# Two masked graph-attention layers: the second layer without complements, every key tile in the form of indicator and mask

## The chip, the cores and the metric

The program runs on one NeuronCore of a Trainium2 chip. Its engines work side by side and each takes its instructions in order: TensorE (PE in the profile, its weight loads PEld), VectorE (DVE), ScalarE (ACT), GpSimd (POOL) and SyncE (SP), which issues the transfers. They wait for one another through semaphores. The metric is the device time of one execution in microseconds, the median of several.

## What is computed

Eight batches of 2048 nodes with 256 features go through two attention layers over one adjacency matrix. The change touches the second layer alone:

```python
q = (h @ W).reshape(B, N, H, D)                       # H = 4 heads, D = 64
e_src = jnp.einsum('bnhd,d->bnh', q, a_src)
e_dst = jnp.einsum('bnhd,d->bnh', q, a_dst)
e = e_src[:, :, None, :] + e_dst[:, None, :, :]
e = jnp.where(e >= 0, e, ALPHA * e)                   # ALPHA = 0.2
e = jnp.where(mask, e, NEG_INF)
attn = jax.nn.softmax(e, axis=2)
h_prime = jnp.einsum('bijh,bjhd->bihd', attn, q)
return jax.nn.elu(h_prime.reshape(B, N, H * D))
...
x = x + _L1_gnn_ref(h, adj, L1_gnn_W, L1_gnn_a)       # h = relu(layernorm(x))
```

## The kernel before

Three blocks run one after the other: the mask is turned and cast, layer 0 works until about 3950 us, then `layer1_block` runs, of which this text tells.

**The idea of layer 1.** The exponential of a leaky ReLU of a sum falls into products: where e_src + e_dst is positive the weight is a factor of the query times a factor b of the key, elsewhere another factor of the query times a factor s of the key. So for each head the kernel needs two masked sums over keys: over the pairs with a positive sum, with q times b, and over the other neighbours, with q times s. Each q row has a column of ones added (E1 = 65 columns), whose sum gives the denominator. TensorE forms both sums; the query factors are multiplied on afterwards.

**Tiles.** A batch `b` has 8 units `m`: head `m // 2`, half `m % 2` of the queries (1024 queries, HT = 8 tiles of 128). A unit has 16 steps `j`, one for each key tile of 128. Eight batches make 64 units and 1024 steps.

**One step.** ScalarE writes `cond` (L1116), which is huge where the sum is positive and 0 elsewhere; two buffers. VectorE takes the minimum with the mask (`pick`, L1277): `u`, 1 for a neighbour with a positive sum; a ring of four buffers. TensorE uses pieces of 128 columns of `u` as stationary operand and the weighted keys as moving one, accumulating in PSUM (`sums`, two sets, one for each half). The weighted keys are float32 values split into a high and a low fp16 part, so each product is done twice.

There are two kinds of key tiles. On an **even** tile VectorE also forms the complement `u2` = mask - u (`rest`, L1285, issued at step j + 1 behind that step's pick). TensorE does per query tile u times b (high, low) and u2 times s (high, low), four matmuls of 65 columns (L1006). On an **odd** tile there is no complement, since (mask - u) s = u (-s) + mask s: two matmuls of 130 columns with u against [b, -s] (L1011) and two of 65 with the mask against s (L1015). Both kinds load 32 stationary tiles a step. A tensor `sign` of 1 and -1 makes s negative on odd tiles (`sign_b`, L1244).

**Building the weighted keys.** For each head VectorE multiplies q by b and by s into `x32` (`weigh`, L1252, at steps 10 and 11), ScalarE rounds to fp16 at step 14 (`high`, L1093 for even tiles, L1094 for odd), VectorE subtracts to get the low parts (`low`, L1260, L1263, at steps 2 and 3 of the next unit) and turns -s back to s for the mask's part (`back`, L1268, step 4). This is done in units m = 6, 7, 0 and 1 for the heads to come.

**What else stands in the loop.** Of the unit before: denominators, `weighted` (the eviction from PSUM, L1326 and L1329, step 8), `value_plus_one` (L1336, step 9), ScalarE's exponential (L1123, step 14, behind `high`), the ELU (L1342, step 14 on VectorE) and the addition to the output (L1350, step 15). In units m = 1 to 5 the projections of the next batch are made in four strips: TensorE transposes at steps 8 and 11 and projects (L975) at 12, 15, 0 and 3, ScalarE copies the results, VectorE takes the statistics. The order is written by hand in the functions `batch` of each engine. VectorE's pick waits for the ring, that is for TensorE's step four before it; ScalarE's comparison waits for the pick two before it. TensorE, VectorE and ScalarE each jump back once a batch (TensorE at L1049).

Of the kernel before, what the change touches and what calls it, by code (L numbers as in the profile page):

```python
# [18 lines left out]
ALU = mybir.AluOpType  # L19
# [4 lines left out]
F16 = mybir.dt.float16  # L24
# [677 lines left out]
PLAIN = 4  # L702
MIXED = 6
PAIRS = NT // 2
# [7 lines left out]
def layer1_block(nc, x1, w, a, out, mask_dram, s_dram, d_dram):  # L712
    with ExitStack() as ctx:
# [39 lines left out]
        sign = sb("sign", [P, NT, H])  # L753
# [7 lines left out]
        u2 = sb("u2", [P, RING // 2, HALF], F16)  # L761
# [5 lines left out]
        v1 = sb("v1", [P, HT, D])  # L767
        e = sb("e", [P, HT, D])
# [35 lines left out]
        u2_ready = sem("u2_ready")  # L804
# [119 lines left out]
        def _(pool):  # L924
# [6 lines left out]
            nc.gpsimd.memset(sign[:, 0:NT:2, :], 1.0)  # L931
            nc.gpsimd.memset(sign[:, 1:NT:2, :], -1.0)
# [18 lines left out]
        def _(pe):  # L951
# [34 lines left out]
            def step(b, m, j):  # L986
# [6 lines left out]
                if j % 2 == 0:  # L993
                    pe.wait_ge(u2_ready, (b * BSTEPS + m * NT + j) // 2 + 1 if isinstance(b, int)
                               else b * (BSTEPS // 2) + (m * NT + j) // 2 + 1)
                else:
                    pe.wait_ge(u_made, RING + n + 1)
                for t in range(HT):
                    group = sums[m % HALVES][:, t // PER_BANK, (t % PER_BANK) * SUM_W:(t % PER_BANK + 1) * SUM_W]
                    cols = slice(t * P, (t + 1) * P)  # L1000
                    ends = j == NT - 1 and (t % PER_BANK == PER_BANK - 1 or t == HT - 1)
                    if j % 2 == 0:
                        for part in range(PLAIN):
                            side = part // 2
                            left = u[:, j % RING, cols] if side == 0 else u2[:, j // 2 % 2, cols]
                            last = nc.tensor.matmul(group[:, side * E1:(side + 1) * E1], left, x_plain[:, h, j // 2, part, :],  # L1006
                                                    start=(j == 0 and t % PER_BANK == 0 and part == 0), stop=False,
                                                    skip_group_check=True)
                    else:
                        for part in range(2):  # L1010
                            nc.tensor.matmul(group[:, :], u[:, j % RING, cols],  # L1011
                                             x_mixed[:, h, j // 2, 2 * part:2 * part + 2, :].rearrange("p k e -> p (k e)"),
                                             start=False, stop=False, skip_group_check=True)
                        for part in range(2):
                            last = nc.tensor.matmul(group[:, E1:SUM_W], mask16[:, j, i0 + t * P:i0 + (t + 1) * P],  # L1015
                                                    x_mixed[:, h, j // 2, 4 + part, :],
                                                    start=False, stop=(ends and part == 1), skip_group_check=True)
# [36 lines left out]
        def _(act):  # L1054
# [123 lines left out]
        def _(dve):  # L1178
# [62 lines left out]
            def sign_b(pb):  # L1241

                dve.wait_ge(ab_done, pb + 1)
                nc.vector.tensor_tensor(b_small[:, :, :], b_small[:, :, :], sign[:, :, :], ALU.mult).then_inc(b_signed, 1)  # L1244

            def weigh(pb, h, side):
                if side == 0:
                    if not (isinstance(pb, int) and pb == 0 and h == 0):
                        dve.wait_ge(x_part_done, 2 * (pb * H + h))
# [7 lines left out]
            def low(pb, h, kind):  # L1257
                if kind == 0:
                    dve.wait_ge(x_high_done, pb * H + h + 1)
                    nc.vector.tensor_tensor(x_plain[:, h, :, 1:PLAIN:2, :], x32[:, 0:NT:2, :, :], x_plain[:, h, :, 0:PLAIN:2, :],  # L1260
                                            ALU.subtract).then_inc(x_part_done, 1)
                else:
                    nc.vector.tensor_tensor(x_mixed[:, h, :, 2:4, :], x32[:, 1:NT:2, :, :], x_mixed[:, h, :, 0:2, :],  # L1263
                                            ALU.subtract).then_inc(x_part_done, 1)

            def back(pb, h):
                dve.wait_ge(x_part_done, 2 * (pb * H + h + 1))
                nc.vector.tensor_scalar(x_mixed[:, h, :, 4:MIXED, :], x_mixed[:, h, :, 1:4:2, :], -1.0, None, ALU.mult)\  # L1268
# [10 lines left out]

            def rest(b, m, j):  # L1280

                n = step_of(b, m, j)
                first = (m % HALVES) * HALF
                dve.wait_ge(u_made, RING + n + 1)
# [181 lines left out]
```

## Time and profile before

| | us |
|---|---|
| median of 3 runs | 5624.24 |
| lowest and highest | 5622.75 and 5629.53 |
| the profiled execution | 5627.96 |
| its span | 5626.0 |
| second layer, first step to the last one's end | 3985.5 to 5616 |
| a middle batch of that layer | 209.8 |
| TensorE busy over the span | 88% |
| VectorE, ScalarE | 67%, 52% |

Busy time says how much of a stretch an engine worked; a line of waits says which engine waited for what. PE's matmuls are pipelined and their ends are modelled, so starts of the weight loads are the firmer measure. PEclk is the granted clock of TensorE: 1.00 is its upper level of 2.4 GHz, 0.5 the lower of 1.2. Where stretches are given below, they begin at the first weight load of a batch or a unit.

### The profile page before, as it was taken

What the parts mean: (1) busy time and instruction counts of PE and PEld (TensorE: products, weight loads), DVE (VectorE), ACT (ScalarE), POOL (GpSimd) and SP (SyncE); (2) the same over time, 40 slices, a digit from 0 to 9 for tenths busy, and PEclk for the clock granted to TensorE, in tenths of its full rate; (3) what the DMA queues carried; (4) which work ended last, traced back from release to release, by engine and by line L of the source; (5) the groups of instructions that cost most, each with busy time, mean ns of one, the idle gap of its engine ahead of it and who ended that gap; (6) DMA issues with size and microseconds to landing.
All of it is one profiled execution on the core that took longest, in us unless ns stands there. A gap on an engine that the chain in (4) does not pass through costs nothing. (4 is left out here: it accounts for less than half of the span.)

```text
span 5626.0 us, 142667 instructions
## 1 busy us (share of the span) xinstructions
PE 4937.7 (88%) x56608; PEld 4468.1 (79%) x56608; DVE 3780.4 (67%) x7098; ACT 2899.5 (52%) x3112; POOL 1323.2 (24%) x1430
## 2 busy tenths in 40 slices
PE   3999799699799969979988996996789889889898
PEld 2898689598689959868977895985689889889888
DVE  3666566566566656656656665664788888888888
ACT  3444344244344424424433442442678778778788
POOL 2133323323323333332333333323000000000000
PEclk6999899899899989989999998998899999999999
DMA  4000000000000000000000000002111111111210
GB/s 177 1 16 8 8 8 15 9 9 8 16 1 16 8 8 9 12 12 9 8 16 1 8 16 8 5 4 81 60 53 47 63 57 43 63 58 42 67 53 33
DMA packets 96262, 159.80 MB, mean 28 GB/s; under 512 B 4977, under 2 KB 87793, under 8 KB 89265
## 3 DMA queue, kind: packets, MB, share of 16 engines
q1 hardware_dynamic: 94768, 141.13, 7.6%
q8 instruction: 434, 7.11, 0.5%
q0 software_dynamic: 896, 10.23, 0.5%
q14 instruction: 164, 1.34, 0.1%
HBM read 109.12 MB, written 38.03 MB: 26 GB/s over the span
## 5 line engine op out<-in xcount | busy, mean ns | idle before, releaser
L451 PEld LDWEIGHTS outs<-v_s,probs 128*128 128x128 f32 x16384 | 1976.4, 192 | 90.7 <-issue 10.4
L451 PE MATMUL outs<-v_s,probs 128*128 128x128 f32 x16384 | 1983.2, 275 | 6.9 <-DVE probs L636 6.9
L516 ACT ACTIVATE slot<-slot,shift 128x1024 f32<-128x1024 f32 x1024 | 1110.7, 1088 | 1381.9 <-PE slot L440 1381.9
L636 DVE SCALAR_TENSOR_TENSOR probs<-slot,bound 128x1024 f32<-128x1024 f32 x1024 | 1250.2, 1224 | 810.0 <-ACT slot L516 808.5
L1116 ACT ACTIVATE cond<-s_all,d_sign 128x1024 bf16<-128x1024 f32 x1024 | 1132.2, 1143 | 274.1 <-DVE u L1277 268.7
L326 POOL TENSOR_TENSOR ctx_sum<-ctx_sum,ctx_part 128x256 f32<-128x256 f32 x896 | 645.4, 725 | 1767.6 <-DVE ctx_part L651 1767.6
L439 PE MATMUL slot<-q_hi,k_hl 128*128 128x512 f32 x2048 | 901.5, 440 | 8.4 <-DVE q_lo L595 8.4
L440 PE MATMUL slot<-q_lo,k_hl 128*128 128x512 f32 x2048 | 801.5, 391 | 0.0
L1277 DVE TENSOR_TENSOR u<-cond,mask 128x1024 f16<-128x1024 bf16 x1024 | 692.2, 684 | 161.7 <-ACT cond L1116 108.9
L1011 PE MATMUL sums<-x_mixed,u 128*128 128x130 f16 x8192 | 800.3, 222 | 0.0
L1006 PE MATMUL sums<-x_plain,u 128*128 128x65 f16 x16384 | 620.7, 196 | 202.5 <-DVE u L1285 157.3
L1015 PE MATMUL sums<-x_mixed,mask 128*128 128x65 f16 x8192 | 772.6, 195 | 0.0
L1006 PEld LDWEIGHTS sums<-x_plain,u 128*128 128x128 f16 x16384 | 571.2, 99 | 236.7 <-DVE u L1285 180.3
L1015 PEld LDWEIGHTS sums<-x_mixed,mask 128*128 128x128 f16 x8192 | 650.2, 99 | 0.0
L1011 PEld LDWEIGHTS sums<-x_mixed,u 128*128 128x128 f16 x8192 | 539.3, 98 | 9.1
L651 DVE TENSOR_TENSOR ctx_part<-outs,inv 128x256 f32<-128x256 f32 x896 | 380.4, 425 | 99.0
L439 PEld LDWEIGHTS slot<-q_hi,k_hl 128*128 128x128 f32 x2048 | 388.3, 190 | 64.5 <-DVE q_lo L595 13.7
L440 PEld LDWEIGHTS slot<-q_lo,k_hl 128*128 128x128 f32 x2048 | 388.7, 190 | 52.5 <-issue 7.5
L1285 DVE TENSOR_TENSOR u<-mask,u 128x1024 f16<-128x1024 f16 x512 | 350.2, 684 | 0.0
L492 ACT ACTIVATE k_hl<-slot,bk_s 64x512 fp32r<-64x512 f32 x128 | 87.3, 682 | 494.6 <-PE slot L376 493.8
L940 POOL TENSOR_TENSOR rstd<-moments,eps 128x4 f32<-128x4 f32 x32 | 16.3, 510 | 1379.3 <-DVE moments L1206 1379.3
L366 PE MATMUL slot<-ident,hs 128*128 128x128 f32 x256 | 56.9, 414 | 315.0 <-DVE hs L558 271.5
(126 smaller groups left out, 4085.5 us busy)
## 6 DMA issues: line engine op xcount, KB each, us to landing
s_all<-s_turned SPq DMA_DIRECT2D x32, 1024.0 KB, 4.7
adj_in<-in_adj SPq DMA_DIRECT2D x16, 1024.0 KB, 6.0
xs<-in_x SPq DMA_DIRECT2D x32, 512.0 KB, 4.5
x<-y SPq DMA_DIRECT2D x32, 512.0 KB, 3.2
x_s<-x SPq DMA_DIRECT2D x32, 512.0 KB, 6.1
o_s<-x SPq DMA_DIRECT2D x16, 1024.0 KB, 5.4
out<-o_s SPq DMA_DIRECT2D x16, 1024.0 KB, 5.7
mask_t<-mask SPq DMA_DIRECT2D x1, 4096.0 KB, 11.1
```

The source lines that it names most:

```text
L326: nc.gpsimd.tensor_tensor(ctx_sum[:, :, h, :], ctx_sum[:, :, h, :], ctx_part[:, h, :, :], ALU.add).then_inc(ctx_added, 1)
L439: nc.tensor.matmul(slot[:, r, :], keys, q_hi[:, h, :], start=True, stop=False)
L440: last = nc.tensor.matmul(slot[:, r, :], keys, q_lo[:, h, :], start=False, stop=True)
L451: last = nc.tensor.matmul(outs[i % OUTS][:, q, :], probs[:, i % PROBS, r, q * P:(q + 1) * P], v_s[:, c * JC + r, h * E1:h * E1 + P], start ...
L516: nc.scalar.activation(slot[:, :, :], slot[:, :, :], ACT.Exp, bias=shift[:, 0:1], scale=SCALE).then_inc(act_done, 1)
L636: nc.vector.scalar_tensor_tensor(probs[:, i % PROBS, :, :], slot_at(s, at(i, has_before))[:, :, :], P_LOW, bound[:, (i // H) % 2, :, :], A ...
L651: nc.vector.tensor_tensor(dst, outs[i % OUTS][:, :, 0:D], inv[:, i % 2, :].unsqueeze(2).to_broadcast([P, IT, D]), ALU.mult).then_inc(ctx_s ...
L1006: last = nc.tensor.matmul(group[:, side * E1:(side + 1) * E1], left, x_plain[:, h, j // 2, part, :], start=(j == 0 and t % PER_BANK == 0 a ...
L1011: nc.tensor.matmul(group[:, :], u[:, j % RING, cols], x_mixed[:, h, j // 2, 2 * part:2 * part + 2, :].rearrange("p k e -> p (k e)"), start ...
L1015: last = nc.tensor.matmul(group[:, E1:SUM_W], mask16[:, j, i0 + t * P:i0 + (t + 1) * P], x_mixed[:, h, j // 2, 4 + part, :], start=False, ...
L1116: nc.scalar.activation(cond[:, j % CONDS, :], s_all[:, h % 2, first:first + HALF], ACT.Relu, bias=d_sign[:, j, h:h + 1], scale=SIGN_SCALE) ...
L1277: nc.vector.tensor_tensor(u[:, j % RING, :], cond[:, j % CONDS, :], mask16[:, j, first:first + HALF], ALU.min).then_inc(u_made, 1)
```

## The change

The even kind of step goes. Every key tile is worked off in the odd form. `rest`, `u2` and the semaphore `u2_ready` are gone, and so is `sign`: s is made negative everywhere. `x_plain` and `x_mixed` become one tensor `x_parts` with six parts for each tile: b high, -s high, b low, -s low, s high, s low. `high` is one instruction, `low` is one, at step 2, and `back` covers all 16 tiles. To make room, `v1` and `e` are no longer tensors of their own but the even and odd rows of `t`.

```diff
-        x_plain = sb("x_plain", [P, H, PAIRS, PLAIN, E1], F16)
-        x_mixed = sb("x_mixed", [P, H, PAIRS, MIXED, E1], F16)
+        x_parts = sb("x_parts", [P, H, NT, PARTS, E1], F16)
...
-        u2 = sb("u2", [P, RING // 2, HALF], F16)
...
-        v1 = sb("v1", [P, HT, D])
-        e = sb("e", [P, HT, D])
+        v1 = t[:, 0:2 * HT:2, :]
+        e = t[:, 1:2 * HT:2, :]
...
-                if j % 2 == 0:
-                    pe.wait_ge(u2_ready, (b * BSTEPS + m * NT + j) // 2 + 1 if isinstance(b, int)
-                               else b * (BSTEPS // 2) + (m * NT + j) // 2 + 1)
-                else:
-                    pe.wait_ge(u_made, RING + n + 1)
+                pe.wait_ge(u_made, RING + n + 1)
...
-                    if j % 2 == 0:
-                        for part in range(PLAIN):
-                            side = part // 2
-                            left = u[:, j % RING, cols] if side == 0 else u2[:, j // 2 % 2, cols]
-                            last = nc.tensor.matmul(group[:, side * E1:(side + 1) * E1], left, x_plain[:, h, j // 2, part, :],
-                                                    start=(j == 0 and t % PER_BANK == 0 and part == 0), stop=False,
-                                                    skip_group_check=True)
-                    else:
...
+                    for part in range(2):
+                        nc.tensor.matmul(group[:, :], u[:, j % RING, t * P:(t + 1) * P],
+                                         x_parts[:, h, j, 2 * part:2 * part + 2, :].rearrange("p k e -> p (k e)"),
+                                         start=(j == 0 and t % PER_BANK == 0 and part == 0), stop=False,
+                                         skip_group_check=True)
+                    for part in range(2):
+                        last = nc.tensor.matmul(group[:, E1:SUM_W], mask16[:, j, i0 + t * P:i0 + (t + 1) * P],
+                                                x_parts[:, h, j, 4 + part, :],
+                                                start=False, stop=(ends and part == 1), skip_group_check=True)
                 last.then_inc(u_used, 1)
...
-                nc.scalar.activation(x_plain[:, h, :, 0:PLAIN:2, :], x32[:, 0:NT:2, :, :], ACT.Copy)
-                nc.scalar.activation(x_mixed[:, h, :, 0:2, :], x32[:, 1:NT:2, :, :], ACT.Copy).then_inc(x_high_done, 1)
+                nc.scalar.activation(x_parts[:, h, :, 0:2, :], x32[:, :, :, :], ACT.Copy).then_inc(x_high_done, 1)
...
-                nc.scalar.activation(e[:, :, :], v1[:, :, :], ACT.Exp, bias=neg_one[:, 0:1]).then_inc(e_done, 1)
+                nc.scalar.activation(e, v1, ACT.Exp, bias=neg_one[:, 0:1]).then_inc(e_done, 1)
...
-                nc.vector.tensor_tensor(b_small[:, :, :], b_small[:, :, :], sign[:, :, :], ALU.mult).then_inc(b_signed, 1)
+                nc.vector.tensor_scalar(b_small[:, :, :], b_small[:, :, :], -1.0, None, ALU.mult).then_inc(b_signed, 1)
...
+            def low(pb, h):
+                dve.wait_ge(x_high_done, pb * H + h + 1)
+                nc.vector.tensor_tensor(x_parts[:, h, :, 2:4, :], x32[:, :, :, :], x_parts[:, h, :, 0:2, :],
+                                        ALU.subtract).then_inc(x_part_done, 1)
...
-                nc.vector.tensor_scalar(x_mixed[:, h, :, 4:MIXED, :], x_mixed[:, h, :, 1:4:2, :], -1.0, None, ALU.mult)\
+                nc.vector.tensor_scalar(x_parts[:, h, :, 4:PARTS, :], x_parts[:, h, :, 1:4:2, :], -1.0, None, ALU.mult)\
                     .then_inc(x_low_done, 1)
...
-                        if j % 2 == 1:
-                            rest(b, m, j - 1)
...
-                        if closed and j in (2, 3):
-                            low(*closed, j - 2)
+                        if closed and j == 2:
+                            low(*closed)
```

On TensorE, an even step and the begin of the odd one behind it stood so before, in the loop over the batches:

```order
L1006 MATMUL sums<-x_plain,u 128x65 [waits u2_ready]
L1006 MATMUL sums<-x_plain,u 128x65 x31
L997 REGISTER_ALU
L1011 MATMUL sums<-x_mixed,u 128x130 [waits u_made]
L1011 MATMUL sums<-x_mixed,u 128x130
L1015 MATMUL sums<-x_mixed,mask 128x65 x2
```

Now a step's last matmuls and the begin of the next one, any two neighbours:

```order
L990 MATMUL sums<-x_parts,u 128x130 x2
L995 MATMUL sums<-x_parts,mask 128x65 x2
L985 REGISTER_ALU
L990 MATMUL sums<-x_parts,u 128x130 [waits u_made]
L990 MATMUL sums<-x_parts,u 128x130
L995 MATMUL sums<-x_parts,mask 128x65 x2
```

The 32 narrow matmuls of the even step, of which the first waited for the complement, have become 16 wide and 16 narrow ones, and each step waits for its own pick alone.

On VectorE, the stretch from step 2 to step 5 of a unit with side work was this (`u<-mask,u` is the complement):

```order
L1277 TENSOR_TENSOR u<-cond,mask 128x1024 [waits u_used,cond_ready]
L1260 TENSOR_TENSOR x_plain<-x,x_plain 128x16x65 [waits x_high_done]
L1277 TENSOR_TENSOR u<-cond,mask 128x1024 [waits u_used,cond_ready]
L1285 TENSOR_TENSOR u<-mask,u 128x1024 [waits u_made]
L1263 TENSOR_TENSOR x_mixed<-x,x_mixed 128x8x130
L1277 TENSOR_TENSOR u<-cond,mask 128x1024 [waits u_used,cond_ready]
L1303 TENSOR_TENSOR den<-sums,a_now 128x12 [waits a_now_done,u_used]
L1306 TENSOR_TENSOR den<-sums,a_now 128x4
L1268 TENSOR_SCALAR x_mixed<-x_mixed 128x8x130 [waits x_part_done]
L1277 TENSOR_TENSOR u<-cond,mask 128x1024 [waits u_used,cond_ready]
L1285 TENSOR_TENSOR u<-mask,u 128x1024 [waits u_made]
```

and is now:

```order
L1252 TENSOR_TENSOR u<-cond,mask 128x1024 [waits u_used,cond_ready]
L1238 TENSOR_TENSOR x_parts<-x,x_parts 128x16x130 [waits x_high_done]
L1252 TENSOR_TENSOR u<-cond,mask 128x1024 [waits u_used,cond_ready] x2
L1270 TENSOR_TENSOR den<-sums,a_now 128x12 [waits a_now_done,u_used]
L1273 TENSOR_TENSOR den<-sums,a_now 128x4
L1243 TENSOR_SCALAR x_parts<-x_parts 128x16x130 [waits x_part_done]
L1252 TENSOR_TENSOR u<-cond,mask 128x1024 [waits u_used,cond_ready]
```

Two complements are gone from these four steps; the two subtractions are one of twice the size at the place of the first, and the sign's turning covers twice the columns.

## Rows read from the trace of the kernel before

**Rows 1.** The page: busy us, share of the span, instructions of each engine.

```profile
PE 4937.7 (88%) x56608; PEld 4468.1 (79%) x56608; DVE 3780.4 (67%) x7098; ACT 2899.5 (52%) x3112; POOL 1323.2 (24%) x1430
```

**Rows 2.** Busy time by stretch, one batch each; columns as headed.

```profile
core 0: us, PE busy (x) PEld busy (x) DVE busy (x) ACT busy (x) POOL busy (x), PEclk, DMA share, GB/s
...
4823.48:5033.32 209.84, 185.48 (x4196) 178.36 (x4197) 180.17 (x351) 164.12 (x194) 8.64 (x8) 0.96 0.17 55
...
5243.57:5445.67 202.10, 185.29 (x4196) 178.20 (x4196) 176.07 (x347) 161.15 (x192) 8.65 (x8) 0.98 0.15 48
5445.67:5616.00 170.33, 160.94 (x4098) 159.28 (x4096) 157.78 (x282) 143.67 (x138) 0.00 (x0) 0.99 0.13 44
```

**Rows 3.** Busy time by stretch, the units of the batch from 4823.48.

```profile
4823.48:4849.68 26.20, 22.86 (x512) 22.23 (x513) 20.63 (x41) 17.98 (x18) 0.00 (x0) 0.89 0.28 93
4849.68:4877.81 28.13, 24.21 (x528) 22.65 (x528) 25.92 (x54) 21.51 (x24) 2.44 (x2) 0.98 0.29 100
...
4927.91:4952.47 24.56, 24.56 (x539) 23.64 (x538) 20.16 (x39) 20.35 (x28) 1.29 (x1) 1.00 0.01 3
...
4975.69:5001.54 25.85, 21.71 (x512) 21.23 (x513) 22.58 (x41) 22.02 (x25) 0.00 (x0) 0.93 0.02 4
5001.54:5033.32 31.78, 20.64 (x517) 19.94 (x515) 25.98 (x43) 22.21 (x22) 0.00 (x0) 0.92 0.29 86
```

**Rows 4.** Busy time by stretch, the fourth unit of the last batch.

```profile
5517.82:5537.45 19.63, 19.63 (x516) 19.63 (x514) 18.59 (x35) 17.84 (x18) 0.00 (x0) 1.00 0.15 57
```

**Rows 5.** Waits, 4903.3 to 4952.5 us: us in total, times, longest.

```profile
DVE u L1277 <- PE sums L1015: 0.4, 1, 0.4
```

**Rows 6.** Waits, 4975.7 to 5001.5 us.

```profile
PEld sums L1006 <- DVE u L1285: 5.8, 5, 2.4
```

**Rows 7.** Waits, 3985 to 5616 us, the second layer.

```profile
PEld sums L1006 <- DVE u L1285: 180.3, 157, 28.4
```

**Rows 8.** TensorE weight loads in order of time: start, us, count.

```profile
5539.91 1.09 PEld L1006 LDWEIGHTS sums<-x_plain,u 128*128 128x128 f16 x32
5540.93 0.13 PEld L1011 LDWEIGHTS sums<-x_mixed,u 128*128 128x128 f16 x2
...
5542.35 1.08 PEld L1006 LDWEIGHTS sums<-x_plain,u 128*128 128x128 f16 x32
```

**Rows 9.** Lines with their count, busy us, mean ns, 3740 to 5626 us.

```profile
L1285 DVE TENSOR_TENSOR u<-mask,u 128x1024 f16<-128x1024 f16 x512 | 350.2, 684 | 0.0
...
L1326 DVE TENSOR_TENSOR t<-sums,rate 128x768 f32<-128x768 f32 x64 | 60.8, 951 | 0.0
...
L1123 ACT ACTIVATE e<-v,neg_one 128x512 f32<-128x512 f32 x64 | 45.3, 708 | 7.1 <-DVE v L1336 7.1
...
L1336 DVE SCALAR_TENSOR_TENSOR v<-t 128x512 f32<-128x512 f32 x64 | 43.8, 685 | 0.0
...
L1252 DVE TENSOR_TENSOR x<-q_s,b_big 128x1040 f32<-128x1040 f32 x32 | 39.5, 1235 | 0.0
...
L1093 ACT ACTIVATE x_plain<-x 128x1040 f16<-128x1040 f32 x32 | 34.5, 1078 | 8.0 <-DVE x L1252 8.0
...
L1094 ACT ACTIVATE x_mixed<-x 128x1040 f16<-128x1040 f32 x32 | 33.5, 1048 | 0.0
...
L1329 DVE TENSOR_TENSOR t<-sums,rate 128x256 f32<-128x256 f32 x64 | 26.5, 414 | 0.0
...
L1268 DVE TENSOR_SCALAR x_mixed<-x_mixed 128x1040 f16<-128x1040 f16 x32 | 13.8, 433 | 0.1
```

**Rows 10.** VectorE in order of time: start, us, what, idle time before it.

```profile
4995.33 0.69 DVE L1342 SCALAR_TENSOR_TENSOR e<-e,v 128x512 f32<-128x512 f32 x1 [1.85 <-ACT e L1123]
...
5597.82 0.69 DVE L1285 TENSOR_TENSOR u<-mask,u 128x1024 f16<-128x1024 f16 x1
5598.43 0.69 DVE L1277 TENSOR_TENSOR u<-cond,mask 128x1024 f16<-128x1024 bf16 x1
```

**Rows 11.** TensorE's jump at the loop's end: duration ns min/median/max.

```profile
L1049 PEldq COMPARE_BRANCH  x7: 83/7632/7990, 4185.2 to 5444.9; - x7
```

More of the change, by code:

```diff
@@ L701 @@
 BATCH_PRO = NS * STRIP_PRO
-PLAIN = 4
-MIXED = 6
-PAIRS = NT // 2
+PARTS = 6
 SUM_W = 2 * E1
@@ L803, in layer1_block @@
         u_made = sem("u_made")
-        u2_ready = sem("u2_ready")
         u_used = sem("u_used")
@@ L930, in _ @@
             nc.gpsimd.memset(eps1[:, :], EPS)
-            nc.gpsimd.memset(sign[:, 0:NT:2, :], 1.0)
-            nc.gpsimd.memset(sign[:, 1:NT:2, :], -1.0)
             nc.gpsimd.memset(ident1[:, :], 0.0).then_inc(consts_ready, 1)
@@ L1001, in step @@
                     ends = j == NT - 1 and (t % PER_BANK == PER_BANK - 1 or t == HT - 1)
-                    if j % 2 == 0:
-                        for part in range(PLAIN):
-                            side = part // 2
-                            left = u[:, j % RING, cols] if side == 0 else u2[:, j // 2 % 2, cols]
-                            last = nc.tensor.matmul(group[:, side * E1:(side + 1) * E1], left, x_plain[:, h, j // 2, part, :],
-                                                    start=(j == 0 and t % PER_BANK == 0 and part == 0), stop=False,
-                                                    skip_group_check=True)
-                    else:
[L1010 to L1017, printed above, removed]
@@ L1248, in weigh @@
                     if not (isinstance(pb, int) and pb == 0 and h == 0):
-                        dve.wait_ge(x_part_done, 2 * (pb * H + h))
+                        dve.wait_ge(x_part_done, pb * H + h)
                     dve.wait_ge(b_signed, pb + 1)
@@ L1255, in weigh @@
                     op.then_inc(x_mul_done, 1)
[L1257 to L1264, printed above, removed]
+            def low(pb, h):
+                dve.wait_ge(x_high_done, pb * H + h + 1)
+                nc.vector.tensor_tensor(x_parts[:, h, :, 2:4, :], x32[:, :, :, :], x_parts[:, h, :, 0:2, :],
+                                        ALU.subtract).then_inc(x_part_done, 1)
             def back(pb, h):
-                dve.wait_ge(x_part_done, 2 * (pb * H + h + 1))
-                nc.vector.tensor_scalar(x_mixed[:, h, :, 4:MIXED, :], x_mixed[:, h, :, 1:4:2, :], -1.0, None, ALU.mult)\
+                dve.wait_ge(x_part_done, pb * H + h + 1)
+                nc.vector.tensor_scalar(x_parts[:, h, :, 4:PARTS, :], x_parts[:, h, :, 1:4:2, :], -1.0, None, ALU.mult)\
                     .then_inc(x_low_done, 1)
@@ L1278, in pick @@
                                         ALU.min).then_inc(u_made, 1)
[L1280 to L1284, printed above, removed]
-                nc.vector.tensor_tensor(u2[:, j // 2 % 2, :], mask16[:, j, first:first + HALF], u[:, j % RING, :],
-                                        ALU.subtract).then_inc(u2_ready, 1)
             def banks(m):
@@ L1335, in value_plus_one @@
                 dve.wait_ge(evicted, HALVES + f + 1)
-                nc.vector.scalar_tensor_tensor(v1[:, :, :], t[:, 0:2 * HT:2, :], 1.0, t[:, 1:2 * HT:2, :], ALU.add, ALU.add)\
+                nc.vector.scalar_tensor_tensor(v1, v1, 1.0, e, ALU.add, ALU.add)\
                     .then_inc(v1_done, 1)
@@ L1341, in elu @@
                 dve.wait_ge(e_done, f + 1)
-                nc.vector.scalar_tensor_tensor(e[:, :, :], e[:, :, :], 1.0, v1[:, :, :], ALU.min, ALU.max).then_inc(elu_done, 1)
+                nc.vector.scalar_tensor_tensor(e, e, 1.0, v1, ALU.min, ALU.max).then_inc(elu_done, 1)
             def finish(b, m):
@@ L1349, in finish @@
                 dve.wait_ge(res_loaded[half], (b + 1) * 16)
-                nc.vector.scalar_tensor_tensor(slab, e[:, :, :], -1.0, slab, ALU.add, ALU.add).then_inc(out_ready, 1)
+                nc.vector.scalar_tensor_tensor(slab, e, -1.0, slab, ALU.add, ALU.add).then_inc(out_ready, 1)
             for k in range(NS):
@@ L1363, in _ @@
                 weigh(0, h, 1)
-                low(0, h, 0)
-                low(0, h, 1)
+                low(0, h)
                 back(0, h)
```

2 lines of the change are left out of this document (removed).

## The prediction

> **What bounds the kernel now.** I read the shares of the engines on the page first, then busy time by batch and by unit of the second layer, then the waits, then single weight loads in order of time. The reader should see in the shares that TensorE leads [rows 1]; but the share is a mean over two layers, and only the second layer is touched. It lasts from 3985.5 to 5616 us, counted from its first step, and consists of eight batches of eight units of 16 steps. A middle batch takes 209.8 us, the seventh 202.1, the last 170.3 [rows 2]. The last one carries no side work for a next batch.
>
> Inside a middle batch the units differ [rows 3]. In the unit that starts at 4927.91 TensorE is busy for all of its 24.56 us, and in the waits of this unit and the one before there is none of TensorE on VectorE; VectorE even waited once for TensorE [rows 5]. In the last batch, from 5517.82 on, a unit takes 19.63 us, busy from end to end, at a granted clock of 1.00, its upper level of 2.4 GHz [rows 4]. These units are limited by TensorE. The others are not: the unit from 4975.69 needs 25.85 us, though it has no projection of the next batch and TensorE would need 19.63. There it waits for L1285, the complement [rows 6]. In the whole layer such waits add up to 180.3 us over 157 times; the longest, 28.4 us, lies before the first step and stays. So 151.9 us of 156 waits are what VectorE costs TensorE today [rows 7].
>
> **The change part by part.** *Even steps get dearer on TensorE.* Read the starts of the weight loads [rows 8]: even step at 5539.91, odd at 5540.93, the next even one at 5542.35. An even step of 32 loads and 32 matmuls of 65 columns takes 1.02 us, an odd one of 32 loads, 16 matmuls of 130 and 16 of 65 columns takes 1.42. Over a unit, 19.63 / 8 = 2.454 a pair, so 1.02 and 1.43. The change makes every step the odd kind. The order of the change repeats exactly this form in every step, so its row is a direct price: 0.41 us more for each of 8 x 64 = 512 even steps, 210 us in all. A fed unit goes from 19.63 to 16 x 1.43 = 22.9 us.
>
> Columns alone say nearly the same: half of the 32 matmuls of an even step grow by 65 columns, 2080 become 3120, and 1040 columns at the 2.4 GHz of the granted clock 1.00 are 0.433 us, 222 us for all. I take the measured 0.41 because it contains the fixed part of each matmul as well; 222 is the upper bound of the term.
>
> *The complement leaves VectorE.* 512 instructions of 684 ns [rows 9], 5.5 us a unit. It was on the path only where TensorE waited for it: at most the 151.9 us come back. What is late next in those units? With the wait gone an even step only needs its own u, and the ring of four u lets VectorE run four steps, 4 x 1.43 = 5.7 us, ahead. VectorE was busy 22.58 us in the unit from 4975.69 and 25.92 in the one from 4849.68 [rows 3]; less 5.5 that is 17.1 and 20.4, against 22.9 for TensorE in the first and 22.9 plus projections in the second. ScalarE is the closer one: 22.02, 22.21 and 17.98 us in the units from 4975.69, 5001.54 and 4823.48 [rows 3], 62.2 together, against 3 x 22.9 = 68.7 plus the loop's jump on TensorE. So both can keep ahead on average.
>
> The hard place is step 14. There ScalarE rounds x32 (1078 + 1048 ns) and takes the exponential (708 ns) before its next comparison [rows 9], and VectorE idled 1.85 us for that, at 4995.33 [rows 10]. Just ahead of it VectorE has the eviction and two products of 1235 ns. From pick 8 to the end of pick 15 I add 8 picks of 0.6 (start to start of instructions that follow closely: 5597.82, 5598.43 [rows 10]), 0.95 + 0.41 + 0.69 + 2 x 1.24 of side work [rows 9], 0.69 for the ELU and about 2 of waiting: 12 us, while TensorE works 8 x 1.43 = 11.4 us. The deficit of under 1 us is covered by the lead of 5.7. I cost the residual waits at 0 to 1 us a batch; if the cover were gone it would be the second rival.
>
> *Smaller pieces.* ScalarE's two roundings of 1040 columns become one of 2080, VectorE's two subtractions (1235 ns as a product of the same size) one; both save one instruction's start. Against it L1268 doubles from 1040 to 2080 columns, 433 ns today [rows 9], so at most 0.43 us more, 32 times, under TensorE's cover in the loop and twice in the open before it: +-1 us. The sign tensor's product of 64 columns becomes one by a constant: nothing. The value plus one, the exponential and the ELU now work inside t: same 512 columns and same engines. They add a reading order but no wait, since the next unit's weighting stands behind them on VectorE; nothing.
>
> *What does not move.* TensorE's jump at the end of a batch, 7.6 us in the median and 7.99 at most, is fetched by its sequencer [rows 11] and is no wait on anyone. The same number of instructions stands in the loop. After it the clock is low: the unit from 4823.48 shows 0.89 [rows 3], of which 0.5 is the 1.2 GHz level, about 2 us lost. Both stay.
>
> **The sum.** By waits: +210 - 152 = +58 us, if only those waits come back. By units it comes out lower. The unit from 4927.91 has one full set of side work: 24.56 - 19.63 = 4.9 us; a batch has four such sets, spread over m = 1 to 5. So what TensorE itself needs of a middle batch is today 8 x 19.63 + 4 x 4.9 + 7.6 + 2 = 186.3 us, and 23.5 of its 209.8 us are lost. I lay the excess over the wait rows to the lower granted clock in starved units (0.93 and 0.92 [rows 3]) and to short waits under each row. The last batch has 170.3 - 157.0 = 13.3 us to give. Lost in all, with the first seven batches taken alike, 7 x 23.5 + 13.3 = 178, so +210 - 178 = +32 us. A middle batch would become 186.3 + 64 x 0.41 = 212.5 us, the last one 183. The unit count stands on measured lengths, the waits on modelled ends; I take +32 and add 9 for waits and clock that do not come back wholly: +41. The profiled execution took 5627.96 us with a span of 5626.0, 3.7 above the median of 5624.24; the difference is added to the median: 5665.
>
> A rule that speaks of this: the Trainium skill (TensorE: Matmul & The Clock Gate, LDWEIGHTS) has a load of 128 columns take 128 / 1.2, an estimate of 107 ns, by the load's columns and not the moving ones. If loads set the pace, wide moving operands would be free. The rows do show loads of 98 ns, but 32 of them start within 1.02 us in an even step and need 1.42 in an odd one, so by the trace the matmuls set the pace. It is the third case below.
>
> **The rivals.** *1. Forecast: TensorE fed throughout,* +41 us, 5665. For it: the units at 24.56 and 19.63 us with TensorE busy throughout, and busy sums of both feeders below 22.9. Between the two sums it spans +25 to +62. Chance 0.78.
>
> *2. The feeders still stall TensorE at step 14.* The complement was only named as last; ScalarE's 2.83 us block at step 14 stays. A wait of up to 2.4 us [rows 6] would stay in the units m = 6, 7, 0 and 1 of a batch: 8 batches x 4 x 2.4 = 77, on top of +32 to +41, so +110 to +118 us, about 5738. Against it: the ring had no chance to fill before step 8 while VectorE was the bound, and now it has. Chance 0.12; a partial form, one such wait a batch, is +20 and lies within the range.
>
> *3. Not slower: the matmul's columns are not what an odd step pays for.* If loads set the pace, or if an odd step's 1.43 us owed something to VectorE's complement, which reads mask and u at the same time, the uniform step would be shorter. For it: in the units of 19.63 us the weight loads are busy from end to end as well [rows 4], so the share alone can't say which of the two binds. It decides where a step falls under 1.43 - 41 / 1024 = 1.39 us; at 3120 columns / 2.4 = 1.30 us the layer gains 0.13 x 1024 = 133 us more and ends at 5665 - 133 = 5532. Loads alone, at 1.02 a step for the even ones as today, would only leave the 178 us that come back, 5446. Against both: odd steps have as many loads as even ones and take 0.4 us longer. Chance 0.05, of which 0.02 within 0.2%.
>
> *4. A mere mis-sizing of recovered time:* little of the clock comes back and boundaries cost more, +62 to +90. Chance 0.05.
>
> **How the numbers follow.** The likeliest case gives 5665. The text's cases put 8 in 10 between 5645 (all lost time back and the jump partly hidden, +21) and 5710 (by waits +58, with one wait of 2.4 us a batch and 222 for the columns). A measurement can tell about 0.2% or 11 us, so slower begins at 5635. Slower: cases 1, 2 and 4 nearly whole, 0.93. Same: the lower tail of case 1 and a share of case 3, 0.04. Faster: 0.03.
>
> **What would show it.** In the profile after, TensorE's waits on VectorE within the layer should shrink from 151.9 us to under 15, VectorE's waits on TensorE should grow to hundreds of us, units of the last batch should take 22.9 us each, and a middle batch 212 to 214. The jump should remain at 7.6 us. If middle batches take over 218 with TensorE idle at steps 13 to 15, case 2 holds. If a unit of the last batch takes 21 us or less, the price of a step was wrong. VectorE's busy time should fall by some 350 us.

## The result and the profile after

| | us |
|---|---|
| before, median of 4 runs | 5626.59 |
| after, median of 4 runs (5658.04 to 5661.8) | 5659.83 |
| ratio, with its 95% interval | 1.006 (1.0042 to 1.0077) |
| span of the profiled execution, before and after | 5626.0 and 5656.2 |

The changed kernel is slower by 33 us in the medians and by 30.2 in the spans; the second layer alone takes 31.4 us more (the eight batches of the view below add up to 1661.9 us, before to 1630.5). The page after, in its line of shares, answers to [rows 1]:

```profile
PE 5102.8 (90%) x56608; PEld 4656.3 (82%) x56608; DVE 3506.7 (62%) x6554; ACT 2899.9 (51%) x3080; POOL 1328.7 (23%) x1428
```

VectorE has lost 544 instructions and 274 us of busy time, TensorE has as many instructions as before and 165 us more. The prediction had said some 350 us for VectorE. It had multiplied 512 complements by 684 ns each, but instructions that follow closely start 0.6 us apart and the page counts their overlap once. Busy time by stretch after, one batch each (us; busy time of PE, PEld, DVE, ACT and POOL with counts; granted clock; DMA share; GB/s), answers to [rows 2]:

```profile
4833.39:5045.54 212.15, 205.13 (x4196) 201.32 (x4197) 145.76 (x283) 163.99 (x191) 9.44 (x8) 0.98 0.17 54
...
5257.17:5461.89 204.72, 204.71 (x4196) 201.04 (x4197) 142.29 (x280) 160.23 (x188) 9.45 (x8) 0.99 0.14 46
5461.89:5645.97 184.08, 184.04 (x4101) 183.91 (x4098) 125.10 (x216) 148.51 (x137) 0.00 (x0) 1.00 0.14 45
```

A middle batch has grown by only 2.3 us (209.84 to 212.15), the last by 13.8 (170.33 to 184.08). The same view by units of that middle batch, and below it one unit of the last batch, shows why; it answers to [rows 3] and [rows 4]:

```profile
4833.39:4857.80 24.41, 24.41 (x512) 24.41 (x513) 16.70 (x31) 17.58 (x17) 0.00 (x0) 0.93 0.27 87
4857.80:4883.47 25.67, 25.67 (x533) 25.33 (x531) 22.28 (x50) 21.64 (x23) 3.68 (x3) 1.00 0.36 115
...
4939.31:4967.20 27.89, 27.89 (x539) 26.96 (x537) 15.52 (x31) 20.57 (x28) 0.00 (x0) 1.00 0.01 3
...
4992.41:5015.37 22.96, 22.96 (x516) 22.96 (x514) 16.13 (x29) 19.93 (x22) 0.00 (x0) 1.00 0.01 3
5015.37:5045.54 30.17, 23.16 (x517) 23.03 (x515) 22.14 (x33) 22.94 (x22) 0.00 (x0) 0.93 0.29 90
```

```profile
5577.00:5599.98 22.98, 22.98 (x517) 22.98 (x515) 14.32 (x26) 18.90 (x18) 0.00 (x0) 1.00 0.01 3
```

Compare unit by unit. The unit that was fed before has grown by 3.33 us (24.56 to 27.89). The unit m = 6, which was starved before, has shrunk, 25.85 to 22.96, and so have m = 1, 28.13 to 25.67, m = 0, 26.20 to 24.41, and m = 7 with the jump, 31.78 to 30.17. In these rows TensorE is now busy from end to end everywhere except at the jump, which stands at the end of m = 7. The waits of the layer, once for the kernel after and once, over the same stretch, for the one before, are (us in total, times, longest):

```profile
PEld sums L990 <- issue: 35.0, 5, 7.1
PEld sums L990 <- DVE u L1252: 6.8, 1, 6.8
```

```profile
PEld sums L1006 <- DVE u L1285: 151.9, 156, 2.4
PEld sums L1006 <- issue: 45.0, 8, 7.7
```

156 waits have become one, and that one is no wait on VectorE's speed: there are six jumps back, five stand under "issue", and the sixth, of the same length, was put down to a pick. The jump itself, which answers to [rows 11] (the shortest of the seven is the end of the loop, without a jump), is a little shorter:

```profile
L1029 PEldq COMPARE_BRANCH  x7: 76/7240/7441, 4188.1 to 5461.2; - x7
```

VectorE in turn now waits for TensorE (one row of the waits after; before, such waits stood on two lines, 32.6 and 18.1 us):

```profile
DVE u L1252 <- PE sums L995: 237.8, 323, 6.4
```

### The profile page after: what moved, and what is told of

Read it like the earlier page. It is cut to its first block and busy times, and to the rows that moved or that the text cites. A ratio compares the mean times of both kernels' runs of the same rounds, so it can differ in the third digit from the quotient of the medians.

```text
span 5656.2 us, 142047 instructions
## 1 busy us (share of the span) xinstructions
PE 5102.8 (90%) x56608; PEld 4656.3 (82%) x56608; DVE 3506.7 (62%) x6554; ACT 2899.9 (51%) x3080; POOL 1328.7 (23%) x1428
## 5 line engine op out<-in xcount | busy, mean ns | idle before, releaser
L990 PE MATMUL sums<-x_parts,u 128*128 128x130 f16 x16384 | 1501.5, 220 | 68.5 <-issue 34.4
L995 PE MATMUL sums<-x_parts,mask 128*128 128x65 f16 x16384 | 1490.0, 194 | 0.0
L995 PEld LDWEIGHTS sums<-x_parts,mask 128*128 128x128 f16 x16384 | 1287.1, 98 | 0.2 <-issue 0.2
L990 PEld LDWEIGHTS sums<-x_parts,u 128*128 128x128 f16 x16384 | 1071.7, 97 | 88.0 <-issue 35.0
L366 PEld LDWEIGHTS slot<-ident,hs 128*128 128x128 f32 x256 | 51.2, 222 | 320.4 <-issue 273.8
L499 ACT ACTIVATE bound<-mask,low 128x1024 f32<-128x1024 uint8 (+1 forms) x256 | 292.2, 1141 | 0.0
L507 ACT ACTIVATE q_hi<-slot,bq_s 128x512 fp32r<-128x512 f32 x128 | 81.0, 684 | 369.2 <-PE slot L397 369.2
```

The source lines that it names most:

```text
L499: nc.scalar.activation(bound[:, c % 2, :, :], mask8[:, c * JC:(c + 1) * JC, bass.ds(strip * STRIP, STRIP)], ACT.Identity, bias=low[:, 0:1] ...
L990: nc.tensor.matmul(group[:, :], u[:, j % RING, t * P:(t + 1) * P], x_parts[:, h, j, 2 * part:2 * part + 2, :].rearrange("p k e -> p (k e)" ...
```

## The experiments

The kernel before was run again beside each group of experiments and took 5624.7 to 5631.05 us. Where a run is compared with the changed kernel below, each is taken as its distance from the kernel before that ran beside it: the changed kernel stands at +33.2. Where a step of a unit is named, the step was found by counting weight loads, 32 a step. The cuts of the code are shortened.

### Without complements, steps left narrow

The kernel before, minus one half of the change:

```diff
-                if j % 2 == 0:
-                    pe.wait_ge(u2_ready, ...)
-                else:
-                    pe.wait_ge(u_made, RING + n + 1)
+                pe.wait_ge(u_made, RING + n + 1)
...
-                            left = u[:, j % RING, cols] if side == 0 else u2[:, j // 2 % 2, cols]
+                            left = u[:, j % RING, cols]
...
-                        if j % 2 == 1:
-                            rest(b, m, j - 1)
```

> The kernel before with the complements left out and nothing else moved: even steps keep their 32 matmuls of 65 columns but use u for both sums, so the second sum of the even tiles is not the reference's. It shows what the removal brings by itself. Theory (178 us of the layer were lost to waits, low clock and short stalls): TensorE needs 186.3 us of a middle batch and 157 of the last, so at most 178 us come back, 5449; ScalarE's 22.0 and 22.2 us in two of the units are then above TensorE's 19.6, some 3 us a batch, so 5470 (5449 to 5485), units of the last batch at 19.6. Rival A (only the 151.9 us of the wait rows come back): 5475 even if ScalarE is no bound. Rival B (ScalarE's block at step 14 goes on stalling TensorE, 2.4 us in four units a batch): 5449 + 77 = 5526 or more.

Measured: 5522.27 us against 5630.18, ratio 0.9809 (0.9792 to 0.9825). That is 108 us less, not 178; the number lies 37 us outside the theory's range and 4 us under rival B. Fed units are as before (24.56, 19.63), but the units m = 6, 7, 0 and 1, in which the weighted keys are built, are not down to what TensorE needs. Busy time by stretch, units m = 1, 6 and 7 of a middle batch:

```profile
4790.65:4815.93 25.28, 23.43 (x532) 22.33 (x530) 21.79 (x47) 21.57 (x25) 2.43 (x2) 1.00 0.33 111
...
4911.52:4932.89 21.37, 19.79 (x517) 19.66 (x515) 15.77 (x29) 19.49 (x23) 0.00 (x0) 1.00 0.03 8
4932.89:4963.69 30.80, 20.58 (x517) 19.93 (x514) 22.92 (x36) 24.50 (x24) 0.00 (x0) 0.95 0.29 87
```

In m = 6 TensorE needs 19.63 us, and ScalarE's 19.49 leave it next to no margin. The waits of the layer name what is late:

```profile
DVE u L1273 <- ACT cond L1112: 246.5, 412, 2.3
...
PEld sums L1007 <- DVE u L1273: 45.6, 51, 2.0
```

With 9.7 us on a second line, TensorE waits 55.3 us for picks, and 38.0 of them lie before step 15, behind ScalarE's block at step 14. In m = 6 it is the only wait, and nearly the whole excess of that unit over 19.63. First VectorE's ELU waits for ScalarE's exponential, then the pick for ScalarE's comparison, then TensorE for the pick (start, us, what, idle time before it):

```profile
4929.66 0.69 DVE L1338 SCALAR_TENSOR_TENSOR e<-e,v 128x512 f32<-128x512 f32 x1 [1.85 <-ACT e L1119]
4930.71 0.69 DVE L1273 TENSOR_TENSOR u<-cond,mask 128x1024 f16<-128x1024 bf16 x1 [0.35 <-ACT cond L1112]
...
4931.45 0.11 PEld L1007 LDWEIGHTS sums<-x_mixed,u 128*128 128x128 f16 x2 [1.71 <-DVE u L1273]
```

This is the stall of the prediction's second rival. So the removal alone is worth 108 us, and narrow steps can't use all that it frees.

### The same with a lighter ScalarE

```diff
-                nc.scalar.activation(cond[:, j % CONDS, :],
-                                     s_all[:, h % 2, first:first + HALF],
+                wide = HALF if isinstance(b, int) and b == 0 and m == 0 and j < 2 else 640
+                nc.scalar.activation(cond[:, j % CONDS, 0:wide],
+                                     s_all[:, h % 2, first:first + wide],
```

> The kernel before without its complements (as e1) and with ScalarE's comparison on 640 of 1024 queries, so the rest keeps old values and the output is not the reference's. It asks why e1 brought 108 us and not 178. Theory (e1 is held back by ScalarE in units m = 6, 7, 0 and 1, where its block at step 14 comes on top of 16 comparisons): each comparison is 0.33 us shorter, 5.2 us a unit, TensorE is fed, 5449 to 5465, and TensorE's waits on the pick (45.6 us in e1) fall under 10. Rival A (VectorE's crowded steps hold it back): 5510 to 5522. Rival B (178 was too much, the clock and the jump cost more than I set): no waits left but 5480 or more.

Measured (two runs): 5485.61 us against 5631.05, ratio 0.9745 (0.9725 to 0.9764). A comparison takes 826 ns in place of 1142. Another 37 us come back, and the waits on the pick fall from 45.6 to 15.8 us on their main line, from 55.3 to 20.8 on both:

```profile
PEld sums L1002 <- issue: 51.6, 11, 8.1
PEld sums L1007 <- DVE u L1274: 15.8, 28, 1.4
```

So ScalarE holds back about half of what was missing. The other half is none of my cases alone. Of the 20.8 us, 13.4 still lie before step 15, since ScalarE's block there is as long as before. Another 7.3 lie before the steps 1, 4 and 6 of m = 1, where VectorE is now the busier of the two (21.81 us, ScalarE 16.95), which is rival A in a small form. "Issue", the jumps above all, is 51.6 us here, 52.5 without the lighter ScalarE and 45.0 in the kernel before. The theory holds in its direction and misses its number by 20 us.

### The changed kernel with idle complements

```diff
+                        if j % 2 == 1:
+                            rest(b, m, j - 1)
...
+            def rest(b, m, j):
+                ...
+                nc.vector.tensor_tensor(u2[:, :], mask16[:, j, first:first + HALF], u[:, j % RING, :], ALU.subtract)
```

> The changed kernel with the 512 complements put back on VectorE at their old places, written to a buffer that nobody reads; TensorE keeps its 16 wide and 16 narrow matmuls a step and waits for the pick alone. (To find the room, wide_s lies inside x32.) It shows whether VectorE's time still counts. Theory (TensorE is the bound and the ring covers the rest): VectorE is back at about 22 us in a unit where TensorE has 22.96, and at 25.9 against 25.67 in unit m = 1; so 5660, at most 5680, units of the last batch at 22.96. Rival (the gain came from VectorE's time as such): some of the 178 us are lost again, 5720 or more.

Measured: 5709.29 us against 5630.18, ratio 1.0141 (1.0125 to 1.0158), 46 us above the changed kernel. The number lies between the two cases: TensorE never waits for these complements themselves, most units keep their length (27.90, 22.97 in the last batch), yet m = 1 and m = 7 of a middle batch take 3.0 and 2.7 us more, and m = 0 and m = 1 of the last one 2.3 and 2.5. Busy time by stretch, unit m = 1 and, lower down, m = 7:

```profile
4885.00:4913.67 28.67, 26.46 (x530) 25.52 (x529) 26.57 (x53) 21.67 (x23) 3.52 (x2) 1.00 0.29 102
...
5046.18:5079.02 32.84, 23.64 (x512) 23.16 (x513) 28.10 (x44) 23.63 (x22) 0.00 (x0) 0.94 0.26 82
```

In m = 1 VectorE is busy for 26.57 us, more than the 25.67 that the unit took without complements, and TensorE waits before the steps 1, 3 and 6. The longest of these waits stands behind the one large subtraction, `low`, which takes VectorE 2.32 us (start, us, what, idle time before it):

```profile
4888.25 2.32 DVE L1239 TENSOR_TENSOR x_parts<-x,x_parts 128x2080 f16<-128x2080 f32 x1
...
4891.22 0.11 PEld L991 LDWEIGHTS sums<-x_parts,u 128*128 128x128 f16 x2 [1.37 <-DVE u L1253]
```

In m = 7 it waits before steps 0, 3, 12 and 15, that is also behind the crowded steps 8 to 11 and behind ScalarE's block, while in m = 0 between the two it waits nowhere but at the jump. I had compared each unit's busy time with TensorE's by itself and left out the waits that VectorE has inside a unit (for ScalarE's block) and the backlog that it carries over a unit's border, as the waits before step 0 and 1 show. So VectorE's relief is needed in the changed kernel too: without it 46 us would come on top of the 33.

### A lead of two steps

```diff
-                dve.wait_ge(u_used, n + 1)
+                dve.wait_ge(u_used, n + 1 + LEAD_CUT)     # LEAD_CUT = 2
```

> The changed kernel with VectorE allowed only two steps ahead of TensorE instead of four (the pick waits for a later step's end). It shows whether the lead is what covers ScalarE's block at step 14 and the crowded steps 8 to 11. Theory (lead covers): two steps are 2.9 us, less than ScalarE's 2.8 us block with the exponential and comparison behind it, and about as much as the two products; TensorE's waits on the pick come back at 1 to 2 us in most units, 5700 to 5760. Rival (lead does not matter, the feeders are simply fast enough): 5660.

Measured: 5718.28 us against 5630.18, ratio 1.0154 (1.0137 to 1.0171), 55 us above the changed kernel. No engine does other work, and 80 waits of up to 1.1 us are there:

```profile
PEld sums L991 <- DVE u L1253: 50.1, 80, 1.1
```

Unit m = 6, the plainest one, goes from 22.96 to 24.51 us:

```profile
5030.38:5054.89 24.51, 23.37 (x512) 23.09 (x513) 16.85 (x33) 21.32 (x23) 0.00 (x0) 1.00 0.02 6
```

This is the theory's case, though the waits stand only in the units that build the weighted keys and just behind them, not in most units. Half of the 50.1 us, 25.1, lies before step 15: ScalarE's block is as long as before; four steps of lead cover it and two don't. Another 16.5 us lie before step 3, behind `low`, and 5.4 before step 12, behind VectorE's crowded steps (one wait before step 15 and one before step 3; start, us, what, idle time before it):

```profile
5053.45 0.11 PEld L991 LDWEIGHTS sums<-x_parts,u 128*128 128x128 f16 x2 [1.14 <-DVE u L1253]
...
5060.14 0.11 PEld L991 LDWEIGHTS sums<-x_parts,u 128*128 128x128 f16 x2 [0.90 <-DVE u L1253]
```

So the lead covers VectorE's own long instruction as well, which the prediction had counted only as a saving.

### Fewer columns at the same number of loads

```diff
+                    if j:
+                        for part in range(4):
+                            left = u[...] if part < 2 else mask16[...]
+                            ...                              # 65 columns for part < 2, else 33
```

> The changed kernel with fewer moving columns in every step but the first of a unit: still 32 weight loads and 32 matmuls, but 16 of 65 and 16 of 33 columns (the wide ones are cut to b alone, the mask's to the last 33), so it leaves out part of both sums. It shows whether columns or loads set the pace of a step. What is read is the time from the first to the last load inside a step, since ScalarE's 1.05 us a comparison will starve such steps as a whole. Now 3120 columns take 1.39 to 1.42 us from first to last load, and 2080 took 0.98. Theory (columns at 2.4 GHz with a fixed part, 0.41 us for 1040): 1568 columns take 0.98 - 0.20 = 0.78. Rival (below the narrow step the loads are the floor): 0.95 or more; then the 0.41 us contained some free columns. The time is that of a kernel bound by ScalarE, 5400 to 5500.

One run, which took 5439.1 us. Weight loads in order of time, the first of a step and one near the end of the same step (start, us, what):

```profile
5402.45 0.11 PEld L994 LDWEIGHTS sums<-x_parts,u 128*128 128x128 f16 x2 [0.26 <-DVE u L1260]
5402.49 0.13 PEld L994 LDWEIGHTS sums<-x_parts,mask 128*128 128x128 f16 x2
...
5403.27 0.12 PEld L994 LDWEIGHTS sums<-x_parts,mask 128*128 128x128 f16 x2
```

From its first to its last load the step lasts 0.85 us at a granted clock of 1.00, between the two expectations (0.78 and at least 0.95). The same measure is 0.98 in the narrow step of the kernel before and 1.41 in the wide one. So 32 loads are no floor at 0.98: the narrow step already pays for its columns, and the widening pays in full. Below that the gain thins out: 512 columns less than in the narrow step saved only 0.13 us where 1040 more cost 0.42. A matmul of 33 columns is followed by the next one's start after 25 to 27 ns, by the trace of this run, where 33 columns at 2.4 GHz are 14 ns.

### Rows of 66

```diff
-        x_parts = sb("x_parts", [P, H, NT, PARTS, E1], F16)
+        x_parts = sb("x_parts", [P, H, NT, PARTS, E1 + 1], F16)
...
```

> The changed kernel with each part of x_parts stored in rows of 66 instead of 65 fp16 values, so that every part starts on a multiple of four bytes; 65 are read as before. Reason: in the mixed kernel a narrow step takes 0.95 us from first to last load, in the kernel before 0.98, and its four parts lie elsewhere in memory. Theory A (a part that starts on an odd pair of bytes costs some 3 to 7 ns a matmul): steps fall from 1.43 by 0.03 to 0.1 us, all 1024 of them: 5560 to 5630. Theory B (the place of the moving operand does not matter): 5660, steps at 1.43.

Measured: 5664.51 us against 5631.05, ratio 1.006 (1.0043 to 1.0077), the same as the changed kernel. Theory A falls: it isn't the two bytes. What makes the narrow step of the mixed kernels a little shorter than the one before stays open.

### Mixed forms

With six parts stored for every tile, each step can take either form. A table says which tiles of a unit get a complement:

```diff
+PLAN = [[], [], [4, 6, 8, 10, 12, 14], [0, 2, ..., 14], [0, 2, ..., 14], [0, 2, ..., 14], [], []]
...
+                if plain:
+                    pe.wait_ge(u2_ready, u2_at(b, m, j) + 1)
+                else:
+                    pe.wait_ge(u_made, RING + n + 1)
...
+            def rest(b, m, j):
+                dve.wait_ge(u_used, RING + n - 1)
+                dve.wait_ge(u_made, RING + n + 1)
...
+                        if j and j - 1 in plan_of(b)[m]:
+                            rest(b, m, j - 1)
```

There is room for one `u2` only, once `wide_s` lies inside `x32`. The table shown is the third one.

> A mixture of both kernels on the new tensor of six parts: complements on the even tiles in units m = 2 to 5 of a batch, where TensorE was the bound, and in all units of the last batch, but only on tiles 0, 2, 4 and 6 in units m = 6, 7, 0 and 1, where VectorE had been. One buffer for the complement, which waits for the step two before. Theory (each narrow step saves TensorE 0.41 us, and costs nothing while VectorE and ScalarE stay below TensorE): against the changed kernel 48 narrow steps a batch, 19.7 us times seven, and about 14 us in the last batch: 5660 - 138 - 14 = 5508, at most 5540 since ScalarE with 22 us comes close in m = 6. Rival (VectorE's crowded steps stall TensorE as soon as complements return): waits as in the kernel before, 5600 or more.

> The mixture again with the narrow steps at other places. In the first mixture TensorE waited 1.2 to 1.6 us for the complement of tiles 0 and 2 in units m = 6, 7, 0 and 1, just behind ScalarE's block at step 14 of the unit before, when the lead is used up. Now they stand at tiles 4, 6 and 8 in m = 7 and 0, at 4 and 6 in m = 1, 2 to 8 in m = 6, 4 to 14 in m = 2, all even ones in m = 3, 4, 5; the last batch likewise, with all even ones from m = 3 on. Theory (a complement is free only where the lead is full): waits for complements fall from 79 to under 30 us; some 36 narrow steps a batch save 14.8 us of the changed kernel's 212, 5660 - 104 - 18 = 5540, at most 5560. Rival (a complement costs its time wherever it stands): about 5585 as the first mixture, or more, since fewer steps are narrow.

> The mixture with complements only where TensorE was the bound: all even tiles in units m = 3, 4 and 5, tiles 4 to 14 in m = 2, none in m = 6, 7, 0 and 1; in the last batch none in m = 0 and 1 and all even ones from m = 3 on. The first two mixtures showed the units m = 6, 7, 0, 1 together at 105.0 and 106.7 us with complements against 103.3 in the changed kernel, so there they return less than they cost. Theory (in those four units a narrow step is no gain, since VectorE is the bound there as soon as it makes complements): 103.3 + 96.4 = 199.7 us a middle batch, the last 166; 5660 - 7 x 12.2 - 18 = 5557, between 5545 and 5570. Rival (the gain of the mixtures came from narrow steps wherever they are): above 5585.

> As h3, with two complements more in m = 6 (tiles 2 and 4) and two in m = 0 (tiles 6 and 8), at places where the lead is full. Theory: if VectorE has some room left there, four narrow steps save up to 1.6 us a batch, 5545 to 5557; if the units from m = 7 on are at VectorE's limit as the first two mixtures suggest, they are paid back in m = 7 and m = 1, 5557 to 5570.

| | complements a middle batch | us | ratio to before |
|---|---|---|---|
| first mixture | 48 | 5584.91 | 0.9921 (0.9905 to 0.9938) |
| second, at later tiles | 42 | 5578.67 | 0.9908 (0.9892 to 0.9925) |
| third, none in m = 6, 7, 0, 1 | 30 | 5555.55 | 0.9879 (0.9862 to 0.9895) |
| fourth, four more than that | 34 | 5562.62 | 0.9885 (0.9869 to 0.9902) |

Waits of the layer in the first, the second and the third mixture (a jump is a wait of about 7 us):

```profile
PEld sums L1018 <- DVE u L1293: 79.1, 96, 2.3
```

```profile
PEld sums L1023 <- DVE u L1285: 47.7, 46, 7.7
PEld sums L1018 <- DVE u L1293: 42.9, 95, 1.1
PEld sums L1023 <- issue: 14.9, 2, 7.7
```

```profile
PEld sums L1023 <- DVE u L1285: 27.2, 4, 7.0
PEld sums L1023 <- issue: 15.3, 2, 7.7
PEld sums L1018 <- DVE u L1293: 7.9, 38, 1.0
```

The first missed its number by 77 us, with 79.1 us of waits on complements. The second missed by 39: the waits on complements fell to 42.9, not under 30, and 17.5 us of waits on picks came up (the row says 47.7, but 30.2 of it are four of the six jumps), and unit m = 1 grew to 27.8 us though it had two complements only. Both had treated each unit as if it stood alone, the mistake that the idle complements show. The third keeps complements out of the four units in which the weighted keys are built. It came out 2 us from its number, and its waits on picks, 27.2 us, are four jumps. Busy time by stretch, units m = 1, 4, 5 and 6:

```profile
4803.50:4829.18 25.68, 25.68 (x533) 25.34 (x530) 22.28 (x50) 21.63 (x23) 3.67 (x3) 1.00 0.37 116
...
4878.99:4903.45 24.46, 24.46 (x539) 23.35 (x538) 20.55 (x40) 20.32 (x28) 1.51 (x2) 1.00 0.01 3
4903.45:4925.59 22.14, 22.10 (x523) 21.09 (x521) 17.80 (x36) 17.19 (x23) 0.00 (x0) 1.00 0.13 37
4925.59:4948.55 22.96, 22.96 (x517) 22.96 (x514) 17.27 (x32) 21.11 (x23) 0.00 (x0) 1.00 0.07 28
```

It has the old length where the old form was fed (24.46 for 24.56) and the new length where the new form is (25.68, 22.96). It is faster than both kernels, by 1.2% than the one before. The fourth gains 0.46 us in m = 6 and pays 1.1 in m = 1 (26.78), as the second half of its expectation has it. There is no complement in m = 1, yet TensorE waits for picks before its steps 1 and 3, which it does not do in the third mixture: the two complements of m = 0 are paid there, and this is the plainest sight of a backlog that crosses from one unit into the next. The two mixtures' ranges overlap, so between them the order is not sure.

## Why the prediction was right

**The bound.** It held that fed units and starved units stand side by side. After the change the fed ones grew by 3.3 us, the starved ones shrank, and no wait on VectorE is left. The relief was also measured apart: taking the complements out of the kernel before returns 108 us, and putting them back into the changed one costs 46.

**The price of a step.** 0.41 us was taken from two kinds of steps in the same trace. Measured, (22.98 - 19.63) / 8 = 0.42 us, 214 us for 512 steps; 210 by the rows and 222 by columns stood in the prediction.

**What comes back.** Here two sums disagreed, 152 by the waits and 178 by lengths of units. With 214 us added and 31.4 left in the layer, 183 came back, so the sum by lengths was right within 5 us. The prediction laid the excess over the wait rows to the lower clock and to short waits. The clock can carry most of it: one minus the granted clock, times the length, summed over the 64 units, is 47 us before and 24 after, an estimate of at most 23 us returned. In unit m = 6 the clock was 0.93 and is 1.00 now. The jumps gave back 2.4 us. Short waits under each named one remain possible, and no run here shows them. A middle batch was forecast at 212.5 and took 212.15, the last at 183 and took 184.1.

**The mis-sized term** is the allowance of 9 us for waits that do not come back. Nothing of it was needed. Without it the forecast had been +32, and +33 was measured. That this is so close is in part luck: the price came out 4 us above its row and the return 5 us above its sum, and the two cancel. The cheaper jump, 7.24 for 7.63 us in the median, is no gain to count on either: with the same work on TensorE it took 7.99 us with the idle complements and 7.88 with a lead of two.

**What is late next.** The prediction said the ring of four covers ScalarE's block. The lead of two shows it: without two of the four steps the kernel loses 55 us, half of the named waits behind that block. It also said that VectorE and ScalarE keep ahead on average; they do, but the run without complements and with narrow steps shows that this depends on the slower step. With narrow steps 108 us come back, with wide ones 183. The wide step is itself a part of the cover: 4 x 1.43 = 5.7 us of lead against 2 x (1.02 + 1.43) = 4.9. It also gives ScalarE a margin in every step, so that the lead fills up again; which of the two does more was not tested. The prediction had counted the lead in wide steps, so it was right, but it treated price and return as two separate terms, and they are not.

**The rivals.** The stall at step 14 (the second) did not appear; the lead of two and the narrow steps without complements show when it does. The third, that loads or VectorE's reading of the same tensors set the pace, falls with the run of fewer columns and with units of 22.98 us, 16 steps of 1.44, although no complement runs beside them. The fourth, less time recovered, did not come: more was recovered than the forecast allowed.

**The Trainium skill's rule** on weight loads (TensorE: Matmul & The Clock Gate, LDWEIGHTS), 107 ns for 128 columns as an estimate, did not decide: the run of fewer columns started 32 loads within 0.85 us, each shown as 96 ns long in the median, so they overlap.

## What to carry to other kernels

Where an engine's units repeat, list them one by one as fed or starved: a dearer step costs in the fed ones, and a relief of the feeder pays in the starved ones up to the new pace and no further. Measure what is lost by the unit's length against the fed unit's, not by the rows of waits alone: they named 152 us where 183 came back, and they leave out the lower clock. And choose the form of a step by the unit it stands in: here either form everywhere was worse than a table that follows the bound, and a feeder's backlog crosses from one unit into the next, so keep extra work off the feeder in the whole stretch around its busiest place.

## What the runs showed of the hardware

- A matmul of 33 columns with its own weight load still takes some 25 to 27 ns from start to start at a granted clock of 1.00; with 65 columns some 29 to 34 and with 130 some 55 to 60 (steps of 1.02 and 1.43 us in the kernel before).
- TensorE's jump back over a loop body of a batch leaves it idle for 6.8 to 7.7 us in the kernels before and after, and the next steps run partly at the lower clock: the unit behind it shows 0.93 after and 0.89 before.
- Starting each moving operand on a multiple of four bytes changes nothing (ratio 1.006 to the kernel before with it and without).
